# Attention scores from two exact pieces in float32r, two heads side by side on half arrays

## The reference

```
qkv = einsum('oc,bchw->bohw', w_qkv, x)
q, k, v = split(qkv.reshape(b, 3 * c, n), 3, axis=1)      # heads 4, d 16, n 3136
attn = softmax(einsum('bhdn,bhdm->bhnm', q, k) * d ** -0.5, axis=-1)
out = einsum('bhnm,bhdm->bhdn', attn, v).reshape(b, c, h, w)
return einsum('oc,bchw->bohw', w_proj, out) + x
```

## Time and profile before

| | us |
|---|---|
| median of 3 runs (8849.29 to 8855.16) | 8852.17 |
| span of the profiled execution, first to last instruction | 8846.4 |
| PE busy | 8390.2 (95%) |
| DVE busy | 7476.4 (85%) |
| ACT busy | 6313.8 (71%) |
| POOL busy | 835.7 (9%) |

### The profile page before, as it was taken

One profiled execution on the slowest core, in us unless ns is written; L12 is line 12 of the kernel. 1 busy time (PEld: TensorE's weight loads), 2 busy tenths in 40 slices (PEclk: granted clock), 3 DMA queues, 4 the chain that ended last, 5 costly groups with the idle time before them and its releaser, 6 DMA issues.

```text
span 8846.4 us, 325856 instructions
## 1 busy us (share of the span) xinstructions
PE 8390.2 (95%) x145926; PEld 4001.2 (45%) x145926; DVE 7476.4 (85%) x9622; ACT 6313.8 (71%) x13874; POOL 835.7 (9%) x676
## 2 busy tenths in 40 slices
PE   4799999999999999999999999999999999999997
PEld 2344444444444444444444444444444444444443
DVE  3789888888888888888888888888888898888885
ACT  1378677776777777677776777777777776777776
POOL 3110101001010010101101010010100101010000
PEclk9799999999999999999999999999999999999998
DMA  1201102020110201102011110201102011020110
GB/s 32 40 14 26 27 18 38 12 38 18 28 27 15 40 15 26 27 13 42 13 26 27 24 33 11 43 16 26 26 15 41 14 26 27 14 42 13 31 20 19
DMA packets 122887, 222.36 MB, mean 25 GB/s; under 512 B 57218, under 2 KB 89090, under 8 KB 121354
## 3 DMA queue, kind: packets, MB, share of 16 engines
q1 hardware_dynamic: 121490, 201.52, 12.5%
HBM read 67.50 MB, written 42.73 MB: 12 GB/s over the span
## 4 chain that ended last, share of the span: by engine, by line
PE 75%; DVE 15%; DMA 4%; SPq 3%; issue 1%; ACT 1%; POOL 0%; POOLq 0%; DVEq 0%; ACTq 0%
PE PS L1248 22%; PE PS L1107 20%; PE PS L1260 19%; DVE small L888 10%; PE PS L1148 3%; PE PS L1168 3%; DVE small L927 1%; PE PS L1200 1%; DMA scratch_att<-o_st 1%; DMA tok_unit<-in_query_ident 1%; PE PS L1138 1%; PE PS L1209 1%; DVE win_scores L930 1%; DMA small<-scratch_att 1%; PE PS L1157 1%
## 5 line engine op out<-in xcount | busy, mean ns | idle before, releaser
L826 ACT ACTIVATE exps<-PS 128x392 f32<-128x392 f32 x12800 | 5488.8, 499 | 2028.4 <-PE PS L1248 1587.7
L888 DVE TENSOR_REDUCE small<-PS 128x1 f32<-128x784 f32 x6400 | 5868.8, 967 | 586.2 <-PE PS L1107 553.1
L1107 PE MATMUL PS<-k_stack,q_stack 96*32 96x392 bf16 x51200 | 3197.9, 334 | 204.4 <-DVE small L888 152.6
L1248 PE MATMUL PS<-q_stack,k_stack 99*32 99x392 bf16 x51200 | 3334.9, 332 | 20.8 <-ACT exps L826 12.7
L1260 PE MATMUL PS<-exps,v_all 128*32 128x392 f32 x25600 | 2665.7, 495 | 0.2 <-ACT exps L826 0.2
L1248 PEld LDWEIGHTS PS<-q_stack,k_stack 99*32 99x32 bf16 x51200 | 1316.3, 95 | 1762.5 <-ACT exps L826 975.1
L1107 PEld LDWEIGHTS PS<-k_stack,q_stack 96*32 96x32 bf16 x51200 | 1182.7, 96 | 1785.3 <-DVE small L888 1092.7
L1260 PEld LDWEIGHTS PS<-exps,v_all 128*32 128x32 f32 x25600 | 760.6, 110 | 355.0 <-ACT exps L826 50.3
L726 POOL TENSOR_TENSOR win_scores<-win_scores,small 128x784 f32<-128x784 f32 x256 | 384.2, 1502 | 1836.5 <-DVE small L939 1836.5
L927 DVE TENSOR_REDUCE small<-PS 128x16 f32<-128x784 f32 x256 | 247.6, 967 | 190.0 <-PE PS L1148 190.0
L1148 PE MATMUL PS<-kmask,tok_unit 113*64 113x392 f32 (+1 forms) x2048 | 376.3, 503 | 18.4 <-DMA tok_unit<-in_query_ident 17.7
(11 more groups left out here) (113 smaller groups left out, 3057.8 us busy)
## 6 DMA issues: line engine op xcount, KB each, us to landing
q_stack<-tok_qk SPq DMA_DIRECT2D x320, 98.0 KB, 3.8
k_stack<-tok_qk SPq DMA_DIRECT2D x320, 98.0 KB, 4.2
kmask<-tok_unit SPq DMA_DIRECT2D x1024, 12.2 KB
att<-scratch_att SPq DMA_DIRECT2D x68, 196.0 KB
z_half<-scratch_z SPq DMA_DIRECT2D x34, 392.0 KB, 7.1
inv_sums<-scratch_rden SPq DMA_DIRECT2D x272, 49.0 KB, 2.1
scratch_att<-o_st SPq DMA_DIRECT2D x512, 26.0 KB
out<-inv_sums SPq DMA_DIRECT2D x68, 196.0 KB, 3.2
```

Of the source, the lines that this page charges most:

```text
L826: nc.scalar.activation(exps(u), PS[:, u % SCORE_BANKS, 0:GTOK], ACT.Exp, scale=D1 ** -0.5).then_inc(s_exps, 1)
L888: nc.vector.tensor_reduce(max_parts[:, n_:n_ + 1], slot(), op=ALU.max, axis=AX.XY)\
L1107: last = mm(PS[32 * r:32 * r + 32, it.bank + j, 0:GTOK], q_stack[0:STACK, stage // 2, q0:q0 + 32], k_stack[0:STACK, stage // 2, chunk * GT ...
L1248: last = mm(PS[32 * r:32 * r + 32, u % SCORE_BANKS, 0:GTOK], k_stack[0:STACK + SHIFT, h, k0:k0 + 32], q_stack[0:STACK + SHIFT, h, c * GTOK ...
```

## The change

Each query and key is cut into two float32 numbers: the first keeps 12 significant bits (the lower bits are masked off with EXACT), the second is the rest. Three products of pieces take the place of six, so a head needs 48 rows of the stack and 2 rows of shift. They are multiplied as float32r. A head then fits on 64 rows, and two heads stand one below the other in the stacks: head 2p on partitions 0 to 49, head 2p+1 on partitions 64 to 113. A stage is now two heads and a quarter of the queries (784 of them, as 2 chunks x 2 heads). There are again 8 stages of 25 tiles. A score unit is one matmul of 128 output partitions on one half of the rows of the array, and units take the two halves in turn. A max step is one tile of queries against 392 keys for both heads, two matmuls on the two halves, and DVE reduces it to two numbers per query. Numbers of units, weigh steps and max steps stay as they were. The bfloat16 copies (L820, piece_m) go away, the cut is made by a mask on DVE and a subtraction on POOL, and the maxima are cut by three DVE operations instead of six. The stacks keep their bytes (half the rows, twice the width), and a stack is loaded for two heads at once. The order strings are written anew, and the table's costs of score and max are other numbers.

```diff
-PIECES = 6
+PIECES = 3
-SHIFT = 3
+SHIFT = 2
+EXACT = 0xFFFFF000 - (1 << 32)
-STAGES = 2 * H1
+PAIRED = H1 // 2
+QUARTERS = GROUPS // 2
+STAGES = PAIRED * QUARTERS
-    "score": (("PE", 167),), "exp": (("ACT", 380),), "weigh": (("PE", 664),),
-    "max": (("PE", 334), ("DVE", 884)), "shift": (("PE", 160), ("DVE", 220), ("SP", 2260)),
+    "score": (("PE", 110),), "exp": (("ACT", 380),), "weigh": (("PE", 664),),
+    "max": (("PE", 200), ("DVE", 884)), "shift": (("PE", 160), ("DVE", 220), ("SP", 2260)),
...
-    "qqqquppvkkttkkopttokkvttkkotptkkotvtjkkottjkkovttjkkottojggggaaaabbaaaabbggzzzzyyyMMMMMMMMMMMMMMMMMMMMMMMMMMMMMM"
+    "qqqqvuppppkkttokkttokkvttjkkottokkvttjkkottokkvttjkkottojggggaaaabbaaaabbggzzzzyyyMMMMMMMMMMMMMMMMMMMMMMMMMMMMMM"
...
-        q_stack = sb("q_stack", [128, H1, PADTOK], bf16)
-        k_stack = sb("k_stack", [128, H1, PADTOK], bf16)
+        q_stack = sb("q_stack", [128, PAIRED, PADTOK], f32r)
+        k_stack = sb("k_stack", [128, PAIRED, PADTOK], f32r)
...
-                    for dst, base, order in ((q_stack, 0, (0, 0, 1, 1, 0, 2)), (k_stack, CH, (0, 1, 0, 1, 2, 0))):
-                        for j, pc in enumerate(order):
-                            sp.dma_start(dst[D1 * j:D1 * j + D1, h, 0:TOKENS],
-                                         pieces[pc][base + D1 * h:base + D1 * h + D1, :]).then_inc(s_stacks[h], 16)
+                    for dst, base, order in ((q_stack, 0, (0, 0, 1)), (k_stack, CH, (0, 1, 0))):
+                        for s in range(2):
+                            c0 = base + D1 * (2 * p + s)
+                            for j, pc in enumerate(order):
+                                sp.dma_start(dst[CH * s + D1 * j:CH * s + D1 * j + D1, p, 0:TOKENS].bitcast(f32),
+                                             pieces[pc][c0:c0 + D1, :]).then_inc(s_stacks[p], 16)
...
-                    nc.vector.tensor_reduce(max_parts[:, n_:n_ + 1], slot(), op=ALU.max, axis=AX.XY)\
+                    nc.vector.tensor_reduce(max_parts[:, :, tile * GROUPS + chunk], slot(), op=ALU.max, axis=AX.X)\
...
-                    nc.vector.tensor_tensor(both_sides(tok_h, it.i), slot(), both_sides(pieces[0], it.i), ALU.subtract)\
-                      .then_inc(s_rest, 1)
+                    nc.vector.tensor_scalar(both_sides(pieces[0], it.i).bitcast(i32), both_sides(tok_h, it.i).bitcast(i32),
+                                            EXACT, None, ALU.bitwise_and).then_inc(s_piece_h, 1)
...
-                    for j in range(2):
-                        chunk = 2 * pair_ + j
-                        for r in range(4):
-                            q0 = tile * 128 + 32 * r
-                            last = mm(PS[32 * r:32 * r + 32, it.bank + j, 0:GTOK],
-                                      q_stack[0:STACK, stage // 2, q0:q0 + 32],
-                                      k_stack[0:STACK, stage // 2, chunk * GTOK:(chunk + 1) * GTOK],
-                                      start=True, stop=True)
+                    for s in range(2):
+                        last = mm(PS[:, it.bank + s, 0:GTOK], q_stack[stacked(s, STACK), p, tile * 128:tile * 128 + 128],
+                                  k_stack[stacked(s, STACK), p, span(chunk)], start=True, stop=True)
...
-                for r in range(4):
-                    k0 = kt * 128 + 32 * r
-                    last = mm(PS[32 * r:32 * r + 32, u % SCORE_BANKS, 0:GTOK], k_stack[0:STACK + SHIFT, h, k0:k0 + 32],
-                              q_stack[0:STACK + SHIFT, h, c * GTOK:(c + 1) * GTOK], start=True, stop=True)
-                last.then_inc(s_scores, 1)
+                mm(PS[:, u % SCORE_BANKS, 0:GTOK], k_stack[stacked(s, STACK + SHIFT), p, kt * 128:kt * 128 + 128],
+                   q_stack[stacked(s, STACK + SHIFT), p, span(chunk)], start=True, stop=True).then_inc(s_scores, 1)
```

More of the change, by code:

```diff
@@ L65 @@
 SWITCH = 100
-SHAPES = {(128, 32): ("score", "max", "weigh", "sum", "wpv"), (128, 64): ("wscore", "wproj", "mlp2"),
-          (64, 128): ("qk", "wval", "mlp1", "gqk", "gv"), (128, 128): ("spread", "wtrans", "gn", "final", "shift")}
+SHAPES = {(128, 32): ("weigh", "sum", "wpv"), (128, 64): ("wscore", "wproj", "mlp2"),
+          (64, 128): ("score", "max", "qk", "wval", "mlp1", "gqk", "gv"), (128, 128): ("spread", "wtrans", "gn", "final", "shift")}
 SHAPE = {kind: shape for shape, kinds in SHAPES.items() for kind in kinds}
@@ L100, in layer0_needs @@
         step(at("xorder", i), at("xload", i))
-        step(at("qk", i), at("xorder", i), *([at("stack", 3)] if attended else []))
+        step(at("qk", i), at("xorder", i), *([at("stack", 1)] if attended else []))
         step(at("spread", i), at("norms"))
@@ L145, in layer0_needs @@
         step(at("gv", k), at("zmid"))
[L146 to L149, removed]
+    left = [at("weigh", QUARTERS * TILES - 1)] if attended else []
+    step(at("stack", 0), *all_of("rest", SIDE), *left)
+    step(at("vcopy", 0), *all_of("gv", 3), *left)
     return needs
@@ L185, in attention_needs @@
     needs[at("store", 0)] += [(at("sums", 0), None), (at("sums", 1), None)]
-    needs[at("stack", 3)] = [(at("sums", 1), None)]
-    needs[at("vcopy", 3)] = []
+    needs[at("stack", 1)] = [(at("sums", 1), None)]
+    needs[at("vcopy", 1)] = []
     return needs
@@ L197, in maxima_needs @@
         first = at("max", *STAGE_MAXIMA[stage][0])
-        if stage in (0, 6) and first in needs:
-            needs[first].append((at("stack", stage // 2 if stage == 0 else 3), None))
+        if stage % QUARTERS == 0 and first in needs:
+            needs[first].append((at("stack", stage // QUARTERS), None))
     return needs
@@ L213 @@
[L213 to L217, removed]
@@ L288, in follow @@
         late = free[e] + (LATE.get(kind, TAIL["SP"]) if e == 4 else TAIL[ENGINES[e]])
-        if kind in SLOTS and part == (2 if kind == "gqk" else 1):
+        if kind in SLOTS and part == 1:
             emptied[step] = late
```

229 lines of the change are left out of this document (115 added, 114 removed).

## The result

The changed kernel takes 9700.18 us (median of 4 runs, 9671.91 to 9767.82), beside 8853.67 us for the kernel before on the same chip: ratio 1.0967, 95% interval 1.0929 to 1.1005. The prediction was 8215 us, range 7900 to 8680. It was wrong in sign.

A forecast was written before the change was run, and what follows sets the result against it. TensorE bounds the kernel (496 of 535 us per image), falling to 435 and leaving DVE (459) as bound at 495 us per image. 365 + 15 x 495 + 370 + 53 = 8213 in span, 8215 us as median; range 7900 to 8680.

The forecast's parts named there:

- Stream and halves: Scores and maxima on TensorE: float32r in one pass, 0.163 us per matmul, halves overlapping; 147 us per image instead of 266.
- One sign: Max steps on TensorE: the two matmuls of a pair should start within 10 ns of each other.
- Rival 3: Scores and maxima: one-pass halves do not overlap at full rate, or float32r takes two passes; 9681 us; chance 0.09.
- loads behind the first hide under a matmul: Weight loads on TensorE: later loads take 0.11 us, less than the 0.163 us stream, so they stay covered.
- 226 added entries into the shape: Entries into 64 x 128 tiles, per image: each pays 0.095 us of uncovered weight load, 21 us together.
- Rival 1: Scores and maxima: waiting steps pay 0.1 us of bare weight load, 300 of 1200 per image; 8603 us; chance 0.26.
- The changes of shape: Tile shape switches on TensorE: 381 more per image at 0.097 us each, 37 us.
- The stacks keep their bytes: Stack loads: bytes unchanged, first stack now two heads; maybe 4 us in the prologue, which the shorter cut gives back.
- DVE at 93%: DVE as the new bound, as loaded as the more loaded engine today: 495 us per image.
- last image: The final image, without layer 0 beside it: from 406 us down to 370 us.
- DVE's need: DVE's work per image: 465.6 us less 6.7 us for shorter cuts and masks, giving 459 us.
- rival 4: TensorE's clock, falling after 4.5 us without matmuls, low a third of the time: 600 us per image, 9868 us; chance 0.05.

The follow-up runs named there:

- small_stack: The changed kernel with every load of a stack cut to its first 392 columns, the rest keeping old values: 9274.00 us, ratio 1.0474 to the kernel before.
- wide_bf16: The changed kernel with scores and maxima in bfloat16 instead of float32r, same 64 x 128 tiles and order: 8948.96 us, ratio 1.0111 to the kernel before.
- The dose: The kernel before plus 3200 tiny matmuls ahead of max steps: same shape 8894.90 us, 64 x 128 in bfloat16 9337.03 us, 64 x 128 in float32r 9607.51 us.
- wide_small: wide_bf16 with every load of a stack cut to its first 392 columns: 8583.30 us, ratio 0.9698 to the kernel before.

## Why the prediction was wrong

**Stream and halves: the mechanism was right.** One pass, 0.33 us in print where the load ran ahead, halves that overlap, 969 ns for the reduction: as said. One sign was not: the two matmuls of a max step start within 10 ns of each other in 42% of the steps only, and 0.13 us apart in the median. Rival 3, whose number (9681) is closest to the result, is refuted in its mechanism.

**The weight load was mis-sized.** The step "loads behind the first hide under a matmul" failed. It compared the load's length (0.11 us) with the stream (0.163 us), but half of the loads do not start during a stream, most of them because they carry the wait for an exponential or a reduction. Only the 226 added entries into the shape were charged. The load is bare in some 530 places of an image, at 0.107 us: 57 us of TensorE, not 21. Rival 1 described this, and its 300 steps beside the 226 entries are nearly the count. Its 520 us per image are too low all the same: small_stack, which has these loads and no wait for the stacks, takes 562, of which 541 would remain at full clock. Why the engines need so much more than the 471 us that TensorE has by this count is open. wide_bf16 shows the price of the format: 751 us.

**The changes of shape were a little oversized.** The prediction charges a pair of changes and one load 0.29 us. The dose shows 0.138 + 0.084 = 0.22.

**The stacks were missed.** "The stacks keep their bytes" is true of the sum over an image, but one load became twice as large at the two moments when nothing covers it. The prediction named the risk only in the prologue and gave it 4 us. It is 366 to 426 us.

**DVE at 93% was not reached.** wide_small has neither of the two costs, and the windows of one of its images say

```profile
3471.40:3991.10 519.70, 492.31 (x4321) 162.29 (x4318) 463.11 (x577) 386.61 (x864) 50.13 (x41) 0.98 0.06 17
```

463.1 us of DVE are 89% of 519.7, not 93%. Against 495 us that is some 23 us for each of 15 images, 345 us, and its last image took 401 us where 370 were forecast. 8215 + 345 + 31 = 8591, beside the 8583 measured. This is bookkeeping and no proof, since the 345 are the measured excess itself: it says only that nothing else of size is missing. Some 7 of the 23 us are the clock by the table below, and 4 are DVE's need, which was put at 459. That a more evenly loaded pair of engines hands over less well is the likely reason for the rest; no run tested it.

**The clock: rival 4's direction.** It makes the other costs larger and is no cause of its own that a run isolates. The same twenty exponentials (661 to 680) in two images of the changed kernel:

```profile
4422.72:4441.09 18.37, 18.37 (x99) 9.78 (x98) 10.33 (x12) 8.66 (x21) 0.00 (x0) 0.50 0.00 1
5014.08:5025.18 11.10, 11.10 (x100) 5.78 (x97) 10.38 (x13) 8.44 (x21) 0.00 (x0) 1.00 0.01 2
```

At 0.50 (1.2 GHz) TensorE is busy throughout and DVE half idle. I cut images 2 to 15 into 40 stretches of twenty exponentials and compared each stretch over the 14 images: a microsecond at 0.50 costs 0.35 us (560 stretches, correlation 0.92). The fastest of the 14 in each stretch, summed, stands for the image at full clock; it is a little too long, since in 3 of the 40 stretches of the changed kernel the clock was low for a time in all 14. This gives a ledger per image:

| kernel | us per image | of it at 0.50 | at full clock |
|---|---|---|---|
| before | 535.4 | 6.3 | 532.9 |
| wide_small | 517.9 | 15.8 | 510.7 |
| wide_bf16 | 541.7 | 40.7 | 529.2 |
| small_stack | 561.8 | 62.4 | 540.5 |
| changed | 588.9 | 98.7 | 559.3 |

So 22 us are gained, float32r's loads cost 30, the waits for the stacks 19, and the lower clock another 27. Rival 4 had the clock low for a third of an image and 600 us per image; it was low for a sixth, and costs some 30 us. Its mean over the span is 0.909 in the changed kernel, 0.954 in wide_bf16, 0.934 in small_stack and 0.972 in wide_small, so it falls less once either cost is gone. The time at 0.50 in three places of an image, in us, says more:

| exponentials | changed | small_stack | wide_bf16 | wide_small |
|---|---|---|---|---|
| 1 to 60 | 34 | 27 | 26 | 9 |
| 461 to 520 | 22 | 25 | 0 | 0 |
| 641 to 700 | 33 | 0 | 11 | 0 |

The third place follows the wait for the first stack, and the clock stays low three times as long with float32r's loads as without. The second goes with the loads alone. The first has a share of each. Most of the clock's 27 us therefore belongs to the loads: small_stack, which has them and no waits, still loses 21, and wide_bf16, which has the waits alone, 12. Why the clock falls at 461 to 520 in some images and not in others is open.

A reading of rival 4 was wrong: 4.5 us is what DVE waited for the sums. TensorE itself was idle for 3.82 us, and its clock fell within them:

```profile
1982.49 0.84 PE L1107 MATMUL PS<-k_stack,q_stack 96*32 96x392 bf16 x8 [3.82 <-DVE small L888]
```

## What to carry to other kernels

A weight load hides only if it may start early: look which instruction carries the step's wait, and charge the full load to every step that waits, not only to the first of a shape. When a buffer is loaded for two users at once, ask for each load what the engines do while it runs, and what may not be overwritten until it has been read; the bytes per image say nothing. A hand-made order is tuned to one set of durations, and moving its letters by a rule cost 450 to 1500 us here, more than the waits it was to remove.

## What the runs showed of the hardware

- Printed weight loads of 128 columns: float32r 182 to 199 ns, bfloat16 93 to 96 ns; uncovered, float32r shows 0.107 us in its matmul and bfloat16 some 0.01 us.
- float32r streams 392 columns in one pass, as bfloat16 does (0.33 us printed in both), and two halves that write the same 128 partitions in different banks overlap: in wide_small four matmuls in a row were through in 0.36 us (2735.705 to 2736.066), where one after the other they would take 0.65.
- A single matmul on another tile shape costs 0.138 us beyond one on the same shape, both changes and a short load included.
- Twelve DMAs of 16 rows and 196 KB each took 17 us to issue from one queue: the first two 0.61 us each, the later ones 1.0 to 2.05. With 392 columns each, all were issued in a median 0.59 us. That earlier transfers still on their way slow the issue is likely and was not tested by itself.
